# Experts' pages taken two at a time with one load of weights, on a decoder layer with 160 experts

## The reference

```python
probs = jax.nn.sigmoid(x @ router_w.T + expert_bias)         # x: 2048 x 256, 160 experts
top_w, top_idx = jax.lax.top_k(probs, 8)                     # 8 experts for each token
top_w = top_w / (jnp.sum(top_w, axis=-1, keepdims=True) + 1e-09) * 2.5
h1 = jax.nn.silu(jnp.einsum('th,eih->eti', x, w_gate))       # 256 -> 128
routed = jnp.einsum('eti,ehi->th', h1 * combine.T[:, :, None], w_down)   # 128 -> 256
shared = jax.nn.silu(x @ w_gate_shared.T) @ w_down_shared.T
```

## Time and profile before

| | us |
|---|---|
| median of three runs | 1020.51 |
| the profiled execution | 1021.68 |
| its span, first to last instruction | 1019.9 |
| `list_entries` begins on DVE | at 539.1 |
| the barrier behind `mix` | at 586.3 |
| `experts`: first rows issued, last rows issued | at 588.1, at 938.3 |
| the barrier behind `experts`, first contributions loaded | at 960.7 |
| mean granted TensorE clock | 0.915 of full speed |

### The profile page before, as it was taken

One profiled execution on the slowest core, in us unless ns is written; L12 is line 12 of the kernel. 1 busy time (PEld: TensorE's weight loads), 2 busy tenths in 40 slices (PEclk: granted clock), 3 DMA queues, 4 the chain that ended last, 5 costly groups with the idle time before them and its releaser, 6 DMA issues. The chain is left out here.

```text
span 1019.9 us, 18292 instructions
## 1 busy us (share of the span) xinstructions
PE 818.2 (80%) x4178; PEld 543.9 (53%) x4178; DVE 509.4 (50%) x1400; ACT 445.7 (44%) x958; POOL 376.3 (37%) x376
## 2 busy tenths in 40 slices
PE   8999999999958989797960078787887877787495
PEld 4443333343334748474640066676776766676284
DVE  1677777877222475757565033343333334333066
ACT  2257776777724252516120034444445444454112
POOL 8000000000000003666677646566666666565200
PEclk9999999999987979998995579999999999999698
DMA  6998787785720102332225579999999999999595
GB/s 232 325 327 264 254 281 278 267 251 213 277 66 21 63 21 86 135 109 95 93 107 191 198 235 305 310 311 321 308 316 315 314 300 294 311 287 295 191 421 212
DMA packets 122058, 234.52 MB, mean 230 GB/s; under 512 B 29416, under 2 KB 61330, under 8 KB 115745
## 3 DMA queue, kind: packets, MB, share of 16 engines
q1 hardware_dynamic: 102720, 196.72, 58.3%
q0 software_dynamic: 17184, 35.20, 9.3%
q10 hardware_dynamic: 2112, 2.10, 0.6%
HBM read 142.80 MB, written 104.46 MB: 242 GB/s over the span
## 5 line engine op out<-in xcount | busy, mean ns | idle before, releaser
L1510 POOL DMA_INDIRECT contributions<-e_y,e_dest x230 | 223.8, 973 | 153.6 <-ACT e_y L1497 117.0
L1430 PE MATMUL e_psg<-e_xt,e_w 128*128 128x128 f32 x920 | 154.7, 294 | 76.9 <-DVE e_xt L1476 70.4
L1646 POOL DMA_INDIRECT row_pool<-rows,places x128 | 129.9, 1015 | 160.2 <-issue 136.3
L1430 PEld LDWEIGHTS e_psg<-e_xt,e_w 128*128 128x128 f32 x920 | 129.8, 204 | 87.7 <-DVE e_xt L1476 80.0
L1476 DVE COPY e_xt<-e_psx 128x256 f32<-128x256 f32 x230 | 97.4, 424 | 146.8 <-PE e_psx L1419 143.4
L497 DVE TENSOR_REDUCE a_mx<-a_psS 128x2 f32<-128x1024 f32 x128 | 152.0, 1218 | 32.7 <-PE a_psS L320 32.6
L455 ACT ACTIVATE a_e<-a_psT 128x512 f32<-128x512 f32 x256 | 138.0, 596 | 54.5 <-PE a_psT L350 52.2
L1490 ACT ACTIVATE e_g<-e_psg 128x128 f32<-128x128 f32 x230 | 63.7, 277 | 214.0 <-PE e_psg L1430 209.9
L1439 PE MATMUL e_psy<-e_w,e_g 128*128 128x256 f32 x460 | 147.5, 405 | 0.0
L1497 ACT ACTIVATE e_y<-e_psy,e_weight 128x256 f32<-128x256 f32 x230 | 108.9, 473 | 47.2 <-PE e_psy L1439 45.0
L1419 PE MATMUL e_psx<-c_ident,e_x 128*128 128x128 f32 x460 | 93.2, 287 | 45.1 <-DMA e_x<-row_pool 45.1
(11 more groups left out here) (214 smaller groups left out, 962.8 us busy)
## 6 DMA issues: line engine op xcount, KB each, us to landing
e_w<-w SPq DMA_DIRECT2D x230, 256.0 KB
row_pool<-fill SPq DMA_DIRECT2D x32, 1260.0 KB, 7.2
e_x<-row_pool SPq DMA_DIRECT2D x230, 140.0 KB
c_c<-contributions SPq DMA_DIRECT2D x16, 1024.0 KB, 15.2
a_k<-k_parts SPq DMA_DIRECT2D x64, 128.0 KB, 3.5
a_q<-q_parts SPq DMA_DIRECT2D x32, 128.0 KB, 4.0
a_q<-q_parts SPq DMA_DIRECT2D x64, 64.0 KB, 3.4
contributions<-e_y,e_dest POOLq DMA_INDIRECT x230
```

Source lines behind the costliest of these rows:

```text
L1430: last = nc.tensor.matmul(psG[:, f.k % 2, 0:n], W[:, f.slot, c * INTER:(c + 1) * INTER], XT[:, f.k % 2, c * n:(c + 1) * n], start=c == 0, ...
L1510: nc.gpsimd.indirect_dma_start(out=contrib, out_offset=bass.IndirectOffsetOnAxis(ap=dest[:, page(f) + k:page(f) + k + 1], axis=0), in_=Y[: ...
L1646: nc.gpsimd.indirect_dma_start(out=pool, out_offset=bass.IndirectOffsetOnAxis(ap=place[:, b, t, k:k + 1], axis=0), in_=rows[:, b, t], in_o ...
```

## The change

The lists now hold pairs and singles. An expert with n pages has n // 2 pairs and, if n is odd, one single (its last page). A half has seven entries, two of them pairs, at places 1 and 4, and nine pages; a pass has 14 entries and 18 pages. Weights are loaded once for an entry. The rows of an entry are loaded with one DMA for each page, since the two pages of a pair don't lie together. The lines of PE, DVE, ACT and POOL already loop over `pages(at)`: a pair is turned by four products, copied out by one copy of 512, gated by products with 256 columns, and gives two tiles of results and two indirect DMAs. The table has 16 numbers for a half: seven experts and nine pages, loaded to registers with two calls. `list_entries` grows, from ten DVE instructions ahead of `spread_done` to 49, into a chain that finds, for each list place, the expert and the numbers of its pages. In `mix`, SP loads weights for 14 entries where it loaded ten.

```diff
-FIRST, MORE = 3, 2
-ENTRIES = FIRST + MORE
-SLOTS = FIRST + MORE
-LISTED = 8
+PAIRS, ONES = 2, 5
+ENTRIES = PAIRS + ONES
+SLOTS = 2 * PAIRS + ONES
+PAIRED = (False, True, False, False, True, False, False)
+LISTED = 16
+PAGES = EXPERTS + UNITS
@@ mix, sync
-                listed = tables.half(h)
+                listed = tables.half(h)[0]
@@ mix, tensor
-                    for i in range(3):
-                        last = nc.tensor.matmul(ps[:, 2, i * P:(i + 1) * P], ones32[:], spread[:, i], start=True, stop=True)
+                    for i in range(7):
+                        bank, place = (2, i) if i < 3 else (3, i - 3)
+                        last = nc.tensor.matmul(ps[:, bank, place * P:(place + 1) * P], ones32[:], spread[:, i], start=True, stop=True)
@@ list_entries
+                    do(nc.vector.tensor_tensor(low[:], starts[:], shifts[:], ALU.subtract))
+                    do(nc.vector.tensor_tensor(high[:], ends[:], shifts[:], ALU.subtract))
...
+                    do(nc.vector.tensor_scalar(pairs_i[:], pages_i[:], 8, None, ALU.arith_shift_right))
+                    do(nc.vector.tensor_scalar(odds_i[:], pages_i[:], 7, 1, ALU.arith_shift_right, ALU.bitwise_and))
...
+                        for bound, found in ((low, opened), (high, closed)):
+                            do(nc.vector.scalar_tensor_tensor(scratch[:], bound[:], nth[:, i:i + 1], own[:], ALU.is_le, ALU.mult,
+                                                              accum_out=found[:, i:i + 1]))
+                            sync()
...
-                    for i in range(3):
+                    for i in range(7):
                         do(nc.vector.tensor_scalar(spread[:, i], ident, listed[:, i:i + 1], None, ALU.mult))
@@ Tables
+        load = lambda a, b, limit: self.nc.values_load_multi_w_load_instructions(
+            self.entry[0:1, bass.ds(h, 1), a:b].rearrange("a h e -> a (h e)"), engines=[mybir.EngineType.SP], min_val=0,
+            max_val=limit, skip_runtime_bounds_check_because="every entry is the number of an expert or of a page")[1]
+        return load(0, ENTRIES, EXPERTS), load(ENTRIES, LISTED, PAGES - 1) if pages else None
@@ experts, sync
-            def load_rows(at, e):
-                n, j = pages(at), COLUMN[at_entry(at)]
-                row = e * P if j < FIRST else LATER + (at_half(at) * MORE + (j - FIRST)) * UNIT
-                sp.dma_start(X[:, page(at):page(at) + n],
-                             pool[bass.ds(row, n * P)].rearrange("(p k) r -> p k r", k=n)).then_inc(x_in[at.slot], 16)
+            def load_rows(at, listed_pages):
+                for k in range(pages(at)):
+                    number = listed_pages[PLACE_OF[at_entry(at)] + k]
+                    sp.dma_start(X[:, page(at) + k], pool[bass.ds(number * P, P)]).then_inc(x_in[at.slot], 16)
```

More of the change, by code:

```diff
@@ L61 @@
 BODIES = 32
-PLACE_OF = COLUMN = (0, FIRST, 1, FIRST + 1, 2)
+COLUMN = tuple(sum(PAIRED[:j]) if PAIRED[j] else PAIRS + j - sum(PAIRED[:j]) for j in range(ENTRIES))
+PLACE_OF = tuple(2 * c if c < PAIRS else PAIRS + c for c in COLUMN)
 LN_EPS = 1e-5
@@ L653, in mix @@
         ends, starts, shifts = (rt(n) for n in ("ends", "starts", "shifts"))
-        within, chosen_row = step1, step2
-        count, total_c, rest, held, grown, limit, shift1, shift2, last_shift, moved, some, firsts_to = (
+        low, high, own, scratch = lg, rank, step1, step2
+        count, total_c, rest, held, grown, limit, shift1, shift2, last_shift, moved, some = (
             sb(f"m_{n}", [P, EXPERTS]) for n in (
[L657 to L660, removed]
+                "count", "total", "rest", "held", "grown", "limit", "shift1", "shift2", "last_shift", "moved", "some"))
+        pairs, odds, pairs_to, odds_to, pairs_from, odds_from, last_page, behind, inside = (
+            sb(f"m_{n}", [P, EXPERTS]) for n in (
+                "pairs", "odds", "pairs_to", "odds_to", "pairs_from", "odds_from", "last_page", "behind", "inside"))
+        units_i, pages_i, pairs_i, odds_i = (sb(f"m_{n}_i", [P, EXPERTS], I32) for n in ("units", "pages", "pairs", "odds"))
+        listed, ready = sb("m_listed", [P, 7]), sb("m_ready", [P, B])
+        turn_of, nth, opened, closed, reach, single = (sb(f"m_{n}", [P, 2]) for n in (
+            "turn_of", "nth", "opened", "closed", "reach", "single"))
+        spread = sb("m_spread", [P, 7, P])
         last_i = sb("m_last_i", [P, 2], I32)
@@ L1173, in list_entries @@
+                    do(nc.vector.tensor_tensor(last_shift[:], last_shift[:], moved[:], ALU.add))
+                    do(nc.vector.scalar_tensor_tensor(behind[:], units_i[:], 0.0, C[:, COL["expert"]], ALU.is_equal, ALU.mult))
                     sync()
[L1174 to L1175 removed]
+                    do(nc.vector.tensor_scalar(pairs_i[:], pages_i[:], 8, None, ALU.arith_shift_right))
@@ L1203, in fill_tables @@
                     dve.wait_ge(tables_spread, 1)
[L1204 to L1210, removed]
+                    halves = EXPERTS // ONES
+                    in_pairs = lambda i: ps[:, 2, i * P:(i + 1) * P].rearrange("p (h a) -> p h a", a=PAIRS)
+                    alone = lambda i: ps[:, 3, i * P:i * P + EXPERTS].rearrange("p (h a) -> p h a", a=ONES)
+                    both = tables.entry[:, :, ENTRIES:ENTRIES + 2 * PAIRS].rearrange("p h (a k) -> p h a k", k=2)
+                    do(nc.vector.tensor_copy(tables.entry[:, :, 0:PAIRS], in_pairs(0)))
+                    do(nc.vector.tensor_copy(tables.entry[:, 0:halves, PAIRS:ENTRIES], alone(0)))
+                    for i in range(2):
+                        do(nc.vector.tensor_copy(both[:, :, :, i], in_pairs(1 + i)))
+                    do(nc.vector.tensor_copy(tables.entry[:, 0:halves, ENTRIES + 2 * PAIRS:], alone(2)))
+                    names = tables.expert[:, :, 0:2 * PAIRS].rearrange("p h (a k) -> p h a k", k=2)
+                    for i in range(2):
+                        do(nc.vector.tensor_scalar(names[:, :, :, i], in_pairs(0), -1.0, float(EXPERTS), ALU.mult, ALU.add))
+                    do(nc.vector.tensor_scalar(tables.expert[:, 0:halves, 2 * PAIRS:], alone(0), -1.0, float(EXPERTS),
+                                               ALU.mult, ALU.add))
                     sync()
@@ L1314, in __init__, with half @@
         self.w_in = [ctx.enter_context(nc.semaphore(f"e_w_in{r}")) for r in range(RING_E)]
[L1316 to L1320, removed]
+    def half(self, h, pages=False):
+        load = lambda a, b, limit: self.nc.values_load_multi_w_load_instructions(
+            self.entry[0:1, bass.ds(h, 1), a:b].rearrange("a h e -> a (h e)"), engines=[mybir.EngineType.SP], min_val=0,
+            max_val=limit, skip_runtime_bounds_check_because="every entry is the number of an expert or of a page")[1]
+        return load(0, ENTRIES, EXPERTS), load(ENTRIES, LISTED, PAGES - 1) if pages else None
     def load_weights(self, sp, w, slot, e):
@@ L1386, in step @@
                 if j == 0:
-                    listed[h] = tables.half(at_half(at))
-                v = listed[h][COLUMN[j]]
+                    listed[h] = tables.half(at_half(at), pages=True)
+                v = listed[h][0][COLUMN[j]]
                 if at.first(RING_E):
```

78 lines of the change are left out of this document (60 added, 18 removed).

## The result

The changed kernel takes 1042.74 us (median of 4 runs, 1040.42 to 1047.39), where the kernel before took 1021.91 beside it (4 runs, 1018.35 to 1024.0): a ratio of 1.0213 [1.0163, 1.0264]. It is 21 us slower, and 987 us (978 to 1007) had been predicted. The profiled execution took 1040.42 us, with a span of 1038.8.

The account below looks back on a forecast made before the run. SP's issuing was taken to bound the expert block, DMA just behind. The terms 5.2 + 2.0 - 52.4 + 11.8 = -33.4 on a profiled 1021.68 gave 988.3, so a median of 987 us (978 to 1007).

Parts of the forecast that it names:

- Two more register loads, one a half: SP's pass in the expert loop: each added load costs 0.60 us, 1.20 a pass (0.6 to 2.8).
- the loop's miss: Expert loop, first to last rows: 290.9 us forecast where 343.3 stood, a change of -52.4.
- Before the loop's first rows: First pass ahead of the loop: eight more pages' rows, 4.1 us, and two more register loads, 1.2, together +5.2.
- SP is the pace: Expert block: SP's issuing sets the time, before and after the change, with the DMA engines just behind.
- Thirteen passes: Expert block: 13 passes where 23 stood, one before the loop and 12 in it; loads of weights fall to 182.
- rival 4: Expert lists: rounding on the chip gives 53 pairs, so fourteen passes, +23.5 us, 1011; chance 0.03.
- a pass of 24.2: Expert loop: SP's issues, boundaries and register loads sum to 24.03 us, 24.2 with 0.18 surplus.
- The barrier: Before the expert block: longer lists and more weight loads make SP 2.4 to 5 us late; +2.0 taken (0 to +8).
- rival 2: Before the expert block: the lists outrun the dispatch or stores and rows queue; barrier +10 us, 995; chance 0.07.
- The end: Last pick to contributions: ten more skipped rounds, 6.7 us, and four more sends by POOL, 5.1, together +11.8.
- Rival 3: Expert loop: the longer body is fetched anew in each of 31 rounds, 59 us, so 1046; chance 0.05.
- Rival 1: Expert loop: nearly full POOL, DMA and SP disturb each other; a pass of 25.4 us, +14, 1001; chance 0.16.

Follow-up runs that it names:

- Run 1: A kernel without the layer, in which SP only loads registers by first number and count: eight from place 0, 4 or 8 some 740 ns, nine from place 7 2084.
- runs 10 and 11: The kernel before with an unneeded second register load a half: loads of 8 and 8 took 1050.01 us, of 7 and 9 1139.09, against 1021.25.
- runs 7 to 9: The changed kernel unaltered (1042.7 us), with one register load of 16 from place 0 a half (992.9), and with two loads of eight (997.1).
- run 8: The changed kernel with one register load of 16 from place 0 a half in place of 7 and 9: 992.9 us, 0.973 of the kernel before.
- run 12: The changed kernel with two register loads of eight, loading only the first 128 of 512 weight columns in the loop: 990.65 us, 0.9699 of the kernel before.
- run 7: The changed kernel again, unaltered: 1042.7 us, 1.0215 of the kernel before.

## Why the prediction was wrong

**The failed step** is the price of the new register loads, in the sentence "Two more register loads, one a half: ... I take 0.60 ... so 1.20 (0.6 to 2.8)". It priced a load by the number of registers and took the 0.53 of the earlier trace rows for anything "close to eight". That row holds for eight numbers from an aligned place, two whole groups of four. The change shifts both: seven numbers leave three over, and nine from place 7 never meet a group. Between 610 and 935 us the 46 loads add up to 73.8 us, 3.21 a half where 0.53 + 0.60 stood, and SP does nothing else meanwhile. Over 23 halves that is 48 us, which accounts for the loop's miss of 46.5. Before the loop's first rows the miss is 4.5. The two halves of the first pass need no experts' numbers from SP, and only the load of nine stands there, 1.88 and 1.89 where 0.53 + 0.60 stood (+1.5). The loop's first half has 3.04 (0.95 and 2.09) where 0.53 stood, since its second load was in no term of the sum (+2.5). The rest, 0.4, are the rows of the eight additional pages and register work, 4.5 where 4.1 stood. Added to the forecast, the 52 us of loads give 1039, and 1042.7 was measured. The upper bound of 2.8 a pass was too low as well, since it was built from whole loads of the aligned kind; the measured addition is some 5.4 a pass (6.42 where 1.06 stands before).

**The rule that was put aside.** The Trainium skill ("Runtime: NRT & Kernel Launch", Instruction fetch mechanics) has about 200 ns a register, and by it 1013 us was worked out and given no weight, because "the load of eight now would take 1.6 us, and the row shows 0.53". The same page of the Trainium skill (The ~15µs preamble/postamble breakdown) speaks of registers loaded from HBM, and the table here lies in SBUF, so its figure is of a neighbour and not of the case itself. Run 1 shows a place for both numbers: 0.2 for each number outside an aligned group, the figure of the Trainium skill, and 0.22 for a whole group of four. One row that contradicted the rule did not refute it for other forms. A rival "the new loads cost 0.2 a number", at 7 x 0.2 + 9 x 0.2 = 3.2 a half, could have been written down, and it makes the change lose. Its sum is the 3.21 that was measured, partly by luck: the seven took 1.03 in the mean, where it has 1.4, and the nine 2.18, where it has 1.8.

**What held, point by point.** SP is the pace: shown for the kernel before by runs 10 and 11, for the changed one by runs 7 to 9 and 12. Thirteen passes: 182 loads of weights and 234 of rows, so rival 4 fell. A second page at 0.53, and a pass of 24.2: so in run 8.

Two terms came out near their numbers by luck, with another engine last than the one forecast. *The barrier*: +1.6 for the +2.0 forecast. SP was to be 2.4 to 5 us late. The tables were first read at 560.9 and not 565, SP then waited 11.5 us for its stores, and it was still 3.2 us early, where it had waited 9.2 and 16.4. So rival 2 fell. In both kernels the barrier opened when POOL was done with its last rows; this wait of POOL's (`DRAIN`, ns, and its start) ended at 586.2 before and at 587.8 after:

```profile
L620 POOLq DRAIN  x1: 20373/20373/20373, 565.8 to 565.8; - x1
```

```profile
L623 POOLq DRAIN  x1: 22292/22292/22292, 565.5 to 565.5; - x1
```

The last rows were sent no later than before (at 579.60, where it was 579.91), and why POOL waits longer behind them is not shown. *The end*: +11.9 for +11.8. POOL's chain was to be last, with 0.67 us for a skipped round on every engine. POOL skips a round in 0.57 us before and in 0.44 after, is through at 952.9 and at 966.3, and then waits for ACT, which waits for PE. First the kernel before, then the changed one:

```profile
956.03 0.97 POOL L1510 DMA_INDIRECT contributions<-e_y,e_dest  x1 [6.12 <-ACT e_y L1497]
```

```profile
954.98 1.03 PE L1506 MATMUL e_psy<-e_w,e_g 128*128 128x256 f32 x4
969.28 1.22 PE L1497 MATMUL e_psg<-e_xt,e_w 128*128 128x128 f32 x4 [13.27 <-issue]
972.72 0.97 POOL L1577 DMA_INDIRECT contributions<-e_y,e_dest  x1 [9.73 <-ACT e_y L1564]
```

PE's chain is last in both. It stops 4.0 us later behind the last rows, stands idle over the skipped rounds for 13.27 us in place of 6.04 (12.7 were forecast), and from POOL's send to the contributions it is 0.7 more, together 11.9; the prediction had 11.1 "by PE".

Rival 3, code loaded anew at each turn, fell: a pass holds nothing but entries and loads, and run 8's turns are as forecast. Rival 1, three full resources, was not borne out: in run 8 DMA is at 0.95 to 0.97 and POOL 95% full, and yet the pass is no longer than forecast; what fullness costs is at most run 12's 6 us. The forecast's direction was wrong, and its model of the loop right: with the one term mended, run 8's profiled execution took 988.53 us where 988.3 had been worked out. That this is so close is luck: the loop was 2.4 us shorter than forecast and the stretch to the end 2.3 longer, though `combine` was to be untouched. Its median is 992.9, against 987.

**The gain, and where it went.** The pairs save SP's time as forecast: 54.8 us in the loop of run 8 (52.4 forecast), and 28 in the whole kernel. The layout of their lists took 50 of it back (run 8 against run 7) on the same queue.

## What to carry to other kernels

When an issuing queue is the pace, price every instruction on it, the register loads too, and price each by its own form: a row of the trace tells what that count at that place costs, not what a neighbour does. Lay out tables that a sequencer reads so that each load starts at a multiple of four numbers and takes whole groups of four, padded if need be; in the loop one load of 16 took 1.19 us in the mean, two of eight 1.25, seven and nine 3.21. And when a sum comes out right, check each term's engine: two of them here had the right size and the wrong engine. If a written rule and a row disagree, look for the case in which each is right before one of them is dropped.

## What the runs showed of the hardware that was not expected

In run 1 a load of registers from a table in SBUF is quick by groups of 16 bytes: four numbers from place 0 take 518 ns and three take 887; eight from place 0, 4 or 8 take some 740 and from place 1, 2 or 7 take 1884. In the loop, loads get longer still: nine from place 7 took 1.88 us before it and up to 2.45 in it. Busy DMA engines are a likely cause, not a shown one: in run 12, with DMA 0.69 busy for 0.94, the loop's 46 loads of eight took 27.4 us for 28.8.

Two chips ran the kernel before in 1167.64 and 1171.12 us and the others in 1020 to 1022, with a granted clock of 0.87 where the others had 0.91, 223 and 241 GB/s in the expert block of the two kernels looked at (308 and 287 elsewhere), and idle time on several engines behind no semaphore. No run here tells the cause.
